# Splitting a weighted sum into three f32r products, and moving half of the last heads' additions to GpSimd

## The reference

```python
# layer 0: latent attention, 32 channels, then attention over 128 concepts
sa  = gamma_sa * w_o(softmax(theta(x)^T phi(x)) g(x)) + x
x   = gamma_moca * w_o(softmax(theta(sa)^T concepts) concepts) + sa
# layer 1 ("the second layer"): queries and keys of 32 channels, values of 256
atten = softmax(q^T k)                  # 1024 x 1024
x   = x + gamma * (v atten^T)           # 256 x 1024
# layer 2: group norm, attention with 256 channels, one head
x   = x + proj(softmax(q k / 16) v)
# layer 3: group norm, 8 heads of 32 channels, layer norm after the projection
x   = layer_norm(wo(concat_h softmax(q_h k_h) v_h)) + x
```

## Time and profile before

| | |
|---|---|
| median of 3 runs | 2846.17 us (2843.23 to 2848.42) |
| the profiled execution | 2845.95 us |
| its span, first to last instruction | 2843.8 us |
| PE / PEld busy | 2609.7 / 1379.6 us |
| DVE busy | 1860.3 us |
| ACT busy | 1207.4 us |
| POOL busy | 273.1 us |
| mean granted TensorE clock | 0.931 |

### The profile page before, as it was taken

How to read it: one execution, slowest core, us unless ns; L and a number is a source line. 1 busy time by engine, 2 the same in 40 slices (tenths; PEclk the granted TensorE clock), 3 DMA queues, 4 the chain that set the end, 5 groups by cost and what they waited for, 6 DMA issues and landing times.

```text
span 2843.8 us, 25566 instructions
## 1 busy us (share of the span) xinstructions
PE 2609.7 (92%) x9636; PEld 1379.6 (49%) x9636; DVE 1860.3 (65%) x1973; ACT 1207.4 (42%) x2073; POOL 273.1 (10%) x138
## 2 busy tenths in 40 slices
PE   7999979989999899998999989998999989978977
PEld 4545644444644456444563545544464445644332
DVE  4533237776577765677566774777657676559986
ACT  3332222626244361634426353362624435232737
POOL 0032110020110202011020201102011020200000
PEclk8999986989999999999999999998999999987989
DMA  2000010100201001010200102011020100122200
GB/s 87 1 0 1 0 45 1 25 21 1 74 1 45 1 30 45 1 45 1 61 14 1 45 1 74 1 23 23 1 74 1 45 1 16 45 45 45 45 1 30
DMA packets 29292, 72.09 MB, mean 25 GB/s; under 512 B 10224, under 2 KB 10416, under 8 KB 28912
## 3 DMA queue, kind: packets, MB, share of 16 engines
q1 hardware_dynamic: 29168, 70.45, 9.9%
HBM read 11.40 MB, written 8.39 MB: 7 GB/s over the span
## 4 chain that ended last, share of the span: by engine, by line
PE 73%; DVE 16%; ACT 4%; issue 3%; SPq 3%; DMA 1%; DVEq 0%; ACTq 0%
PE ps L744 14%; PE ps L630 11%; PE ps L597 11%; PE ps L616 9%; PE ps L907 7%; PE ps L829 6%; DVE fa_nmx L1273 3%; PE ps L605 3%; DVE ba_nmx L1273 3%; SPq L483 2%; PE ps L686 2%; DVE accb L1435 2%; PE ps L815 2%; DVE bb_nmx L1273 1%; PE ps L826 1%
## 5 line engine op out<-in xcount | busy, mean ns | idle before, releaser
L1273 DVE TENSOR_REDUCE ba_nmx<-ps 128x1 f32<-128x1024 f32 x448 | 531.9, 1219 | 205.5 <-PE ps L616 204.1
L1126 ACT ACTIVATE prb<-ps 128x512 f32<-128x512 f32 x896 | 490.4, 600 | 350.0 <-PE ps L630 328.0
L1435 DVE TENSOR_TENSOR accb<-accb,prb 128x1024 f32<-128x1024 f32 x336 | 402.3, 1218 | 121.9 <-ACT prb L1126 121.5
L744 PE MATMUL ps<-pr,h 128*128 128x512 f32 x896 | 433.7, 607 | 0.7
L997 ACT ACTIVATE pr<-ps 128x512 f32<-128x512 f32 x336 | 195.5, 598 | 480.6 <-PE ps L829 270.6
L630 PE MATMUL ps<-qs,ks 97*128 97x512 f32 x896 | 371.1, 490 | 8.7 <-ACT prb L1126 8.6
L616 PE MATMUL ps<-ks,qs 96*128 96x512 f32 x896 | 356.4, 503 | 15.6 <-DMA ks<-part 8.4
L630 PEld LDWEIGHTS ps<-qs,ks 97*128 97x128 f32 x896 | 168.0, 204 | 265.1 <-ACT prb L1126 175.2
L907 PE MATMUL ps<-prb,vb 128*32 128x512 f32 x1792 | 252.6, 637 | 2.3 <-ACT prb L1126 2.2
L616 PEld LDWEIGHTS ps<-ks,qs 96*128 96x128 f32 x896 | 175.3, 203 | 158.5 <-issue 97.1
L1273 DVE TENSOR_REDUCE fa_nmx<-ps 128x1 f32<-128x1024 f32 x168 | 198.7, 1216 | 80.8 <-PE ps L815 56.4
(11 more groups left out here) (300 smaller groups left out, 3010.0 us busy)
## 6 DMA issues: line engine op xcount, KB each, us to landing
qs<-part SPq DMA_DIRECT2D x168, 128.0 KB, 2.4
ks<-part SPq DMA_DIRECT2D x168, 128.0 KB, 2.4
xm<-in_x SPq DMA_DIRECT2D x8, 1024.0 KB, 5.8
out<-prb SPq DMA_DIRECT2D x28, 256.0 KB, 2.2
q2k<-part SPq DMA_DIRECT2D x48, 128.0 KB, 2.4
w<-in_weights SPq DMA_DIRECT2D x1, 2592.0 KB, 8.7
out<-pr SPq DMA_DIRECT2D x4, 256.0 KB, 2.0
qs<-ba_nmx_r SPq DMA_DIRECT2D x56, 4.0 KB, 1.8
```

Of the source, the lines that this page charges most:

```text
L744: mm = pe.matmul(o.ps[:, 2 + ch, :], o.v[:, jt, tile(ch)], o.pr[:, t % 4, :], start=jt == 0, stop=jt == NT - 1)
L1126: act.activation(weights3(o, s, g), o.ps[:, turn3[score_use(s, g) % 3], :], ACT.Exp)\
L1273: dve.tensor_reduce(o.nmx[:, head, it:it + 1], o.ps[:, bank:bank + 2, :], AX.XY, ALU.max, negate=True).then_inc(o.max_sb[n].sem, 1)
L1435: dve.tensor_tensor(o.sums[pair], o.pairs[(s - 1) % 2][pair] if j == 1 else o.sums[pair], o.pairs[s % 2][pair], ALU.add).then_inc(done.sem, 1)
```

## The change

It has three parts.

1. In layer 1, `weigh` makes three f32r products per channel tile in place of one f32 product. The values are split into `v_hi` (ACT) and `v_lo` (DVE, the value minus `v_hi`), each in two halves of 128x1024. Each step's weights are split too: ACT copies `pr` into `p_hi` (rounded to f32r), and POOL subtracts it from `pr` into `p_lo`. Both have three buffers. `weigh` now runs three steps behind the scores, not two, and waits for POOL's `p_lo`. ACT's copy of step t waits for the weighing of step t - 3.
2. In layer 3 of the last two batches (6 and 7), POOL makes the additions of the second pair of heads, 14 per round. DVE keeps those of the first pair.
3. All the lists of `ORDER` are new.

```diff
+            o.v_hi, o.v_lo = tokens(o.ql2), tokens(o.kh2)
+            o.p_hi = [o.kl2[:, 0, 0:IW], o.kl2[:, 0, IW:], o.kl2[:, 1, 0:IW]]
+            o.p_lo = [o.kl2[:, 1, IW:], o.qh2[:, 1, 0:IW], o.qh2[:, 1, IW:]]
...
+        def both_add(b):
+            return b >= B - 2
...
+                def low_part(b, t):
+                    pool.wait_ge(o.p_hi_sb.sem, o.p_hi_sb.at(b, t + 1))
+                    pool.tensor_tensor(o.p_lo[t % 3], o.pr[:, t % 4, :], bf32(o.p_hi[t % 3]), ALU.subtract)\
+                        .then_inc(o.p_lo_sb.sem, 1)
...
+                            for t in (2 * (4 * ic + jg), 2 * (4 * ic + jg) + 1):
+                                if n == 1:
+                                    low_part(b, t)
+                                    yield
                             add_pair(b, n, 4 * ic + jg)
...
                 def back(b):
                     yield "head"
+                    for n in range(IC * CH if both_add(b) else 0):
+                        for j in range(1, NT):
+                            s = NT * n + j
+                            pool.wait_ge(o.exped[3].sem, o.exped[3].at(b, QUAD * (s + 1)))
+                            if j == 1 and n:
+                                pool.wait_ge(o.total[3].sem, o.total[3].at(b, n))
...
+                            pool.tensor_tensor(o.sums[1], o.pairs[(s - 1) % 2][1] if j == 1 else o.sums[1],
+                                               o.pairs[s % 2][1], ALU.add).then_inc(done.sem, 1)
...
-                            mm = pe.matmul(o.ps[:, 2 + ch, :], o.v[:, jt, tile(ch)], o.pr[:, t % 4, :],
-                                           start=jt == 0, stop=jt == NT - 1)
+                            for values, weights in ((o.v_hi, o.p_hi), (o.v_hi, o.p_lo), (o.v_lo, o.p_hi)):
+                                mm = pe.matmul(o.ps[:, 2 + ch, :], values[:, jt, tile(ch)], weights[t % 3], ...)
...
+                    behind = 3 if n == 1 else 2
...
+                        if n == 1:
+                            act.wait_ge(o.exped[1].sem, o.exped[1].at(b, t + 1))
+                            if t >= 3:
+                                act.wait_ge(o.weighed[1].sem, o.weighed[1].at(b, t - 2))
+                            act.activation(o.p_hi[t % 3], o.pr[:, t % 4, :], ACT.Copy).then_inc(o.p_hi_sb.sem, 1)
...
-                            for pair in range(2):
+                            for pair in range(1 if both_add(b) else 2):
```

More of the change, by code:

```diff
@@ L125 @@
     ("backs", "SP"): (
-        6, 6, 1, 1, 9, 2, 1,),
+        6, 6, 8, 1, 2, 2, 1,),
 }
@@ L318, in front_lane @@
             o.l0_wo = made["wo"]
-            made = in_turn("l0_act", {"theta": 1, "parts": IC, "e2": 1, "p2t": 1})
+            made = in_turn("l0_act", {"theta": 1, "parts": IC, "e2": 1, "p2t": 1, "v_hi": 2, "p_hi": STEPS})
+            o.v_hi_sb, o.p_hi_sb = made["v_hi"], made["p_hi"]
+            o.p_lo_sb = in_turn("p_lo", {1: STEPS})[1]
             o.l0_theta, o.l0_parts, o.l0_e2, o.l0_p2t = made["theta"], made["parts"], made["e2"], made["p2t"]
@@ L552, in back @@
                     yield "head"
+                    for n in range(IC * CH if both_add(b) else 0):
[4 more added lines that the diff above has]
+                                pool.wait_ge(o.total[3].sem, o.total[3].at(b, n))
+                            done = o.summed3[1]
+                            if j > 1:
+                                pool.wait_ge(done.sem, done.at(b, (NT - 1) * n + j - 1))
+                            pool.tensor_tensor(o.sums[1], o.pairs[(s - 1) % 2][1] if j == 1 else o.sums[1],
+                                               o.pairs[s % 2][1], ALU.add).then_inc(done.sem, 1)
+                            yield
                 return front, back
@@ L739, in weigh @@
                         ic, jt = divmod(t, NT)
-                        pe.wait_ge(o.exped[n].sem, o.exped[n].at(b, t + 1))
+                        if n == 1:
+                            pe.wait_ge(o.p_lo_sb.sem, o.p_lo_sb.at(b, t + 1))
+                        else:
+                            pe.wait_ge(o.exped[n].sem, o.exped[n].at(b, t + 1))
                         if jt == 0 and ic:
@@ L743, in weigh @@
                         for ch in range(CH):
-                            mm = pe.matmul(o.ps[:, 2 + ch, :], o.v[:, jt, tile(ch)], o.pr[:, t % 4, :],
-                                           start=jt == 0, stop=jt == NT - 1)
+                            if n == 2:
+                                mm = pe.matmul(o.ps[:, 2 + ch, :], o.v[:, jt, tile(ch)], o.pr[:, t % 4, :],
+                                               start=jt == 0, stop=jt == NT - 1)
+                                continue
+                            for values, weights in ((o.v_hi, o.p_hi), (o.v_hi, o.p_lo), (o.v_lo, o.p_hi)):
+                                mm = pe.matmul(o.ps[:, 2 + ch, :], values[:, jt, tile(ch)], weights[t % 3],
+                                               start=jt == 0 and weights is o.p_hi and values is o.v_hi,
+                                               stop=jt == NT - 1 and values is o.v_lo)
                         mm.then_inc(o.weighed[n].sem, 1)
@@ L758, in chunks @@
                         yield
-                        if t > 1:
-                            weigh(t - 2)
+                        if t >= behind:
+                            weigh(t - behind)
                             yield
@@ L764, in chunks @@
                             yield
-                    for t in (STEPS - 2, STEPS - 1):
+                    for t in range(STEPS - behind, STEPS):
                         weigh(t)
@@ L991, in exps @@
                         act.wait_ge(o.weighed[0].sem, o.weighed[0].at(b, s - 1))
+                    if n == 2 and t >= 4:
+                        act.wait_ge(o.weighed[n].sem, o.weighed[n].at(b, t - 3))
                     if n and t >= 4:
-                        act.wait_ge(o.weighed[n].sem, o.weighed[n].at(b, t - 3))
                         ic, jg = divmod(s - 2, 4)
@@ L1029, in chunks @@
                         yield
-                        if t == NT + 1:
+                        if n == 1:
+                            act.wait_ge(o.exped[1].sem, o.exped[1].at(b, t + 1))
+                            if t >= 3:
+                                act.wait_ge(o.weighed[1].sem, o.weighed[1].at(b, t - 2))
+                            act.activation(o.p_hi[t % 3], o.pr[:, t % 4, :], ACT.Copy).then_inc(o.p_hi_sb.sem, 1)
+                            yield
+                        if t == (NT + 2 if n == 1 else NT + 1):
                             take(0)
@@ L1084, in front @@
                     yield from to_stacks(b, 1, True)
-                    take_values(b, 1, 0, o.v, 2)
-                    yield
+                    for half in range(2):
+                        act.wait_ge(o.v_ps[1].sem, o.v_ps[1].at(b, half + 1))
+                        act.activation(o.v_hi[:, 4 * half:4 * half + 4, :].rearrange("p (k a) c -> p k a c", a=2),
+                                       o.ps[:, 2 - 2 * half:4 - 2 * half, :].rearrange("p k (a c) -> p k a c", a=2),
+                                       ACT.Copy).then_inc(o.v_hi_sb.sem, 1)
+                        yield
                     shift_row(b, 1, o.qs01, ROW)
@@ L1395, in front @@
                     yield from low_stacks(b, 1, True)
-                    take_values(b, 1, 1, o.v, 0)
-                    yield
+                    for half in range(2):
+                        dve.wait_ge(o.v_hi_sb.sem, o.v_hi_sb.at(b, half + 1))
+                        rows = slice(4 * half, 4 * half + 4)
+                        dve.tensor_tensor(o.v_lo[:, rows, :].rearrange("p (k a) c -> p k a c", a=2),
+                                          o.ps[:, 2 - 2 * half:4 - 2 * half, :].rearrange("p k (a c) -> p k a c", a=2),
+                                          bf32(o.v_hi[:, rows, :]).rearrange("p (k a) c -> p k a c", a=2), ALU.subtract)\
+                            .then_inc(o.v_sb[1][half].sem, 1)
+                        yield
                     yield from maxima(b, 1, 1)
```

24 lines of the change are left out of this document (13 added, 11 removed), and 44 rows, old and new, of the table ORDER.

## The result

The changed kernel takes 2817.55 us (median of 4 runs, 2815.2 to 2820.61), the kernel before 2844.82 (4 runs, 2843.23 to 2848.42). The ratio is 0.9899, 95% interval 0.9887 to 0.9911: about 27 us faster. The forecast was 46 us. The direction was right and the time lies within the range of 2768 to 2838 us, but the gain is 0.6 of the forecast, and the time is one that rival A had named (2814 to 2830 us).

The account below looks back on a forecast made before the run. PE was taken to bound layer 1 and DVE the middle part of "backs". From 2845.95 us, layer 1 gives -32 (-39.7 products, +8 values) and layer 3's additions -14: 2800 us, range 2768 to 2838.

Parts of the forecast that it names:

- rival A: Last stage: the path DVE and POOL share takes back the gain; 2814 to 2830 us, chance 0.18.
- D: Layer 1: f32r products stall on weight loads, so only the last stage changes; 2840 us, chance 0.04.
- B: Layer 1: POOL's subtraction bounds the chunk, slower than before from 2.2 us a step; 2874 us, chance 0.09.
- if PE is the bound throughout: Layer 1 products: condition for saving 0.31 us in each of 128 steps, 39.7 us in all.
- The 1.0 us for the values: Layer 1: DVE's low part waits for ACT's high part, costing 1.0 us per batch, 8 us in all.
- let order and POOL's load cancel: Layer 1: 0 to 2 us a round from the order, set against part of PE's 10 us lost in "fronts".
- Beside the maxima the forecast was 191 us: Last stage: 155 us of DVE work, 20 of waits for POOL and 16 idle, against 223 before.
- A's threshold: Last stage: a mean wait of 0.97 us per DVE addition, from which the stage gains nothing.
- the prediction's own last line: Prediction wrong if rounds don't shrink, or steps without maxima take less than 3.4 or more than 4 us.
- there the two engines alternate, 21 x 3.6: Last stage without maxima: DVE and POOL take turns, 76 us for 21 additions, 83 us with chunk starts.
- C: Last stage reaches PE's floor (-36 us), each round regains up to 2 us; 2778 down to 2766, chance 0.13.
- Sign (5) of the prediction: Last stage: POOL's additions may show some 0.5 us more than 2.36 each.

Follow-up runs that it names:

- e7: Changed kernel, but from batch 2 on POOL makes one more subtraction per step, of 320 columns, into an unread buffer: 2874.48 us in one run.
- e2: Changed kernel, but layer 1 makes one f32 product of the high parts, low parts made and left out: 2839.78 us, ratio 0.9986.
- e3: Changed kernel, but POOL subtracts only 64 of 512 columns per step, except the first three steps of batches 0 and 1: 2815.87 us.
- e1: Changed kernel, but DVE makes all 56 additions of the second pair of heads again, in the new order: 2820.74 us, ratio 0.9909.
- e4: Changed kernel, but POOL's additions take only 32 of 512 columns per head, all waits kept: 2787.62 us, ratio 0.9793.
- e5: Changed kernel, but POOL adds only in chunks beside maxima (three of batch 6's four, two of batch 7's): 2802.6 us, ratio 0.9843.
- e8: Kernel before, layer 1 and old lists kept (POOL's own is new), with POOL making the second pair's additions in batches 6 and 7: 2878.74 us.
- e6: Changed kernel, but batches 0 and 1 keep the single f32 product and the first part's old lists: 2811.76 us, ratio 0.9882.

## Why the prediction was right or wrong

**The products' own time: right.** Six records take 1.38 us (forecast 1.41) and POOL's subtraction 1.29 (forecast 1.27). A chunk, from PE's first score to its last column sum, takes 47.5 us in the mean of the six rounds, before 51.7 (forecast 47 against 52). D falls with the first number, B with the second, and e7 shows that B comes true at 2.08 us already, below its forecast 2.2.

**The size of a round: the right number, partly for another reason.** A round is 5.0 us shorter, forecast 4 to 5. The forecast had 5 from the products less 1 for the values, and nothing from the order. By e2 it is 2.3 from the products and 2.7 from the rest of the change. The step that failed here is "if PE is the bound throughout": the 0.34 us saved in each of 128 steps are 43 us, and by e2 only 22 us of them arrive. What the other 21 are lost to, no run shows. That the size of the round came out is luck. The gain around the group norm, 1.9 us, was named, with 0 to 2 us, and set off against a loss elsewhere. The 1.0 us for the values did not show: from the first maximum of layer 1 to its first score PE needs 14.6 to 14.8 us, before 15.1.

**"Fronts": the first term that was wrong.** The sum took layer 1's gain for all 8 batches, so 8 us here, and let order and POOL's load cancel. It is 4.4 us longer. The 78 us of POOL work in 108 us were seen, but not that they are crowded into the first half: POOL's timeline there shows no gap between these instructions.
```profile
163.15 1.26 POOL L554 TENSOR_TENSOR qs<-prb,ks 128x512 fp32r<-128x512 f32 x1
164.37 1.29 POOL L554 TENSOR_TENSOR ks<-prb,ks 128x512 fp32r<-128x512 f32 x1
165.62 2.52 POOL L554 TENSOR_TENSOR q2k<-pr,q2k 128x512 fp32r<-128x512 f32 x2
168.10 2.99 POOL L554 TENSOR_TENSOR qs<-prb,ks 128x512 fp32r<-128x512 f32 x2
```
With e3's short subtraction the stage takes 438.5 us, 4.4 below before. So layer 1 in sum was -27 by PE's records, not -32.

**"Backs": the step that failed.** Forecast -14, measured 0: this is rival A, and the time lies in its range. The milestones, in us, are read from PE's records: from the end of the sixth round to the start of the last maximum tile's last matmul, from there to the start of batch 7's last column sum, and from there to the end of the stage.
```
                last maximum   last sum   end
before          261.4          65.5       22.3
after           236.6          89.1       23.1
e1 (DVE adds)   254.9          74.4       22.3
e4 (short)      226.4          71.8       22.2
e5 (beside)     237.4          74.4       22
e8 (old order)  274.3          83.0       24
```
Beside the maxima the forecast was 191 us against 223, and it is 201. Its terms, from the table of stretches, for line L1496, for line L1328 (the maxima) and for line L1503 (the scaling of the heads' sums, two SBUF inputs), and L1503's counterpart in e1:
```profile
2506.00:2707.00 201.00, 62.86 (x35) 0.88 0.14 32
2506.00:2707.00 201.00, 111.84 (x95) 0.88 0.14 32
2506.00:2707.00 201.00, 3.80 (x4) 0.88 0.14 32
```
```profile
2497.00:2716.00 219.00, 2.73 (x4) 0.84 0.13 30
```
The 35 additions take 62.9 us, 1.80 each, forecast 1.7: the wait is 0.62 us each, forecast 0.57. That it came out is luck in part: 14 of the 35 additions were held up, not 0.65 of them, and by 1.5 us each, not by 0.87. The maxima are untouched (1.18). The waits so cost 2 us more than forecast.

The rest of the miss is not POOL's in the main. All other work takes 180.2 - 62.9 - 111.8 = 5.5 us, where 1.4 stood in the sum, and the idle time is 20.8, not 16; but in e1, where POOL adds nothing, the same two terms are already 197.7 - 81.8 - 112.0 = 3.9 and 219 - 197.7 = 21.3 us. So the idle time came with the new order, and of DVE's other instructions the four of L1503 lost 1.1 us to POOL. A's threshold, 0.97 us of wait, was not reached here. (The 1.4 was no measure of DVE's other work either. Neighbouring records overlap; by its records that work is 7.0 us before and 10.4 after, 2.6 of the difference in four more instructions that read PSUM.)

Behind the maxima the forecast was 83 against 65, and it is 89 to 91. The alternation was foreseen, and its step nearly. DVE's timeline and POOL's, in the same stretch:
```profile
2731.53 6.73 DVE L1496 TENSOR_TENSOR accb<-accb,prb 128x1024 f32<-128x1024 f32 x2
2738.18 3.39 DVE L1496 TENSOR_TENSOR w<-w,pr 128x1024 f32<-128x1024 f32 x1
2741.50 3.40 DVE L1496 TENSOR_TENSOR accb<-accb,prb 128x1024 f32<-128x1024 f32 x1
```
```profile
2737.13 3.35 POOL L585 TENSOR_TENSOR w<-w,tmp 128x1024 f32<-128x1024 f32 x1
2740.46 6.64 POOL L585 TENSOR_TENSOR accb<-accb,prb 128x1024 f32<-128x1024 f32 x2
```
Each engine's record now lasts 3.3 to 3.4 us, for 1.17 and 2.36 us of work: both wait in turn, and one step takes 3.32 us from start to start (forecast 3.6). By the prediction's own last line, 3.4 to 4 us, that is a miss, if a near one.

But only 8 of the 21 additions that start in this part last over 3 us; their mean is 2.18 us, a wait of 0.97, which is A's threshold. Over both parts the mean is 1.95 us, between the 1.7 of the forecast and the 2.1 of A. So "there the two engines alternate, 21 x 3.6" is the step that failed: by the measured step it would be 21 x 3.32 + 7 = 77 us, and 12 to 14 us more passed, in which neither engine is full (DVE is busy for 59.1 and POOL for 58.9 of 91 us). One thing that the sum lacked is what else stands in DVE's queue, for instance the final scaling:
```profile
2774.08 2.86 DVE L1552 SCALAR_TENSOR_TENSOR prb<-prb,vec,xm 128x512 f32<-128x512 f32 x1
2776.86 3.38 DVE L1496 TENSOR_TENSOR w<-w,acc 128x1024 f32<-128x1024 f32 x1
```
0.75 us of work takes 2.86. Three such instructions (L1503, L1548, L1552) are held up in this part and take 5.9 us more than in e1. The chain that ended last runs through the scaling, and through an addition further on:
```profile
2774.16 2.79 DVE prb L1552
2786.87 3.39 DVE w L1496
```
Against e1, where DVE adds alone, POOL's additions lose 89.1 - 74.4 = 15 us here. Part of it is PE's own: its granted clock in this part is 0.89 with POOL's additions and 1.00 in e1, and it is busy for 77 us in place of 68. No run separates the two. The new order itself makes this part 9 us longer and the one ahead of it 6.5 us shorter (e1 against before).

By the spans, 21 us of the forecast 46 did not come: 13.6 in "backs"; 4.6 in layer 1, where "fronts" missed its share by 12.4 and the six rounds beat their 24 by 7.8; and 2.8 in the later start, which is scatter. By the medians it is 19.

The Trainium skill, "SBUF — State Buffer", section "Who interferes with whom", says that VectorE and GpSimd share a port pair under an exclusive lock, that a VectorE instruction with two SBUF inputs contends with a GpSimd instruction that reads SBUF, and that a reduction such as the maxima does not. With that the pair of timelines agrees (3.32 us a step, where 1.17 and 2.36 us one after the other would be 3.5), and so do the maxima (1.18 us beside POOL too). The price per meeting in the one row that the forecast used, 0.87 us, was a short one: beside the maxima it is 1.5 us in the mean.

Of C, one half came true: each round regained 1.9 us of idle time by the new order (up to 2 were given). The other half did not: "backs" came nowhere near PE's floor even in e5 (334 us against 314). Sign (5) of the prediction was right: POOL's additions take 2.84 us in the mean, 0.5 more than 2.36.

Still open: why e8's part beside the maxima lost 13 us (expected at most 12 in all). Its DVE list was not rearranged in a run, so that additions in a row are the cause is argued from the timeline, not shown. How the order and the products share a round is known from e2 alone, in which PE's work no longer fits the lists.

## What to carry to other kernels

Before work moves to GpSimd, write down for the stretch what else VectorE does there: if it reads PSUM it can fill GpSimd's time, if it reads two SBUF tiles both engines take turns and a step costs nearly the sum of the two (3.32 us here for 1.17 and 2.36). Move it only in stretches of the first kind (e5: 15 us better than moving all of it), and make that decision per stretch, also for load: the same split that is hidden in the rounds binds in the first part (e3, e6). Sum up every instruction of the kind that collides, not only the one that is edited. And look for the idle time on both sides of a moved instruction: the gap at the group norm went from 7.0 to 0.44 us, but 4.68 us of it had only moved ahead of three matmuls.

## What the runs showed that was not expected

- Two engines in turn show it in both records: 3.35 and 3.4 us for 2.36 and 1.17 us of work, without any idle time between them. A busy share then says nothing: in e8 DVE does less and is busy for longer.
- An edit that is worth some 3 us at most in one order (e1, not clear of the scatter) costs 32 in another (e8).
- POOL writes f32r about as fast as f32: 1.29 us for a subtraction of 128x512, against 1.26 for the addition in the earlier trace rows.
- TensorE's clock went with the additions of two other engines: with POOL's short or gone behind the maxima, the granted clock there is 1.00 (e1, e4, e5), so 2.4 GHz throughout, and PE is busy for 67.5 of 72 to 68.3 of 75 us. With them PE waits more often (busy for 77.2 of 91 us) and the mean is 0.89, so it fell to the lower level, 1.2 GHz, for part of the time. One such fall comes with an idle time of 3.38 us that ends at 2747 us: from 2744 to 2762 us the mean is 0.81, and the eight projection matmuls (L632) there take 5.64 us on the chain that ended last, where the same eight take 3.63 in e1.
